# Up products with standing weights in fp32, read per block from memory, in place of split products with standing rows

## The chip, the cores and the metric

The kernel runs on one core of one Trainium2 chip. The metric is device time in microseconds (us), the median of several runs; a profiled execution gives the rows quoted below. TensorE is called PE, VectorE DVE, ScalarE ACT, GpSimd POOL, SyncE SP. A "block" is 128 token rows that one expert processes.

## What is computed

A cross attention is followed by a mixture of experts (8 experts, the best 2 for each token). Batch 16, 256 queries, 1601 keys, width 128, hidden width 256.

```python
x = x + attention(layernorm(x) @ Wq + bq, ctx @ Wk + bk, ctx @ Wv + bv, mask)
xn = rms_norm(layernorm(x), norm_scale)
weights, idx = softmax(top_k(xn @ w_router.T, 2))
up = xn @ w_up[idx].T            # [rows, 512], halves u and gate
h = u * silu(gate)
down = h @ w_down[idx].T         # [rows, 128]
x = layernorm(x) + sum(down * weights) + x
```

## The kernel before

**Two stages.** 32 units (128 queries of one batch each) of attention run first, in slots that interleave scores, exponentials, turns of the probabilities and products with the context. Each token's normalized row goes to memory twice, scattered by POOL into `rows_in`, one region for each expert (`scatter`, L570). Then NB = 71 blocks of 128 rows are read back, each from one expert's region; DVE works out the tables of which block belongs to which expert. The first 41 blocks (FULL) come from the first 24 units and can start before the last units are done. The last four slots of attention stand between the steps of blocks 0, 2, 5 and 8 (`LATE_SLOTS`).

**One step of the second stage**, in the order written for PE in `step(m)`: turn the rows of block m+1 (L1505), up products of block m (L1532), turn the hidden values of block m-2 (L1549), down products of block m-3 (L1560). PE takes the expert number of a block from a register and so addresses that expert's weights among all eight, which stay on the chip.

The up product stands the turned rows and moves 512 columns of weights, three times in the fast one-pass type (F32R): high rows by high weights, high rows by low weights, low rows by high weights. ACT makes the high part of the rows (L809) and DVE the low part (L1265). The weights were split in the same way once for each expert during attention (ACT L795, DVE L1036), from `wup_in`. After the up product ACT takes the tanh of the gate half (L819), DVE makes the hidden values in two instructions (L1287, L1292), PE turns them, ACT copies them out (L825), PE makes the down product, ACT scales it with the gate (L832) and POOL scatters it to `parts` (L643, semaphore `s_sent`).

**Order of the other engines.** Each engine runs its instructions in the order written. On DVE the tables for the second phase stand after the work of blocks 14 (`table_all`), 16 (`table_owners`) and 17 (`table_starts`), `find_places` after block 12. POOL has, between the sends of results, the last scatters of the attention: three before the send of block 6 and four before that of block 11.

**SP** issues the transfers: `load_block(m)` (L469) into a ring of XR = 12 buffers, so it first waits for `s_sent` of block m-12; after blocks 29 to 36 also `fill_end` (L447), and after blocks 64 to 69 the six loads of parts (`load_parts`, L483, 512 KB each), of which the first waits for the results of blocks 44 to 55. Every fourth block SP first loads four row numbers into registers (L465). At the end the last results are gathered, added and stored.

Of the kernel before, what the change touches and what calls it, by code (L numbers as in the profile page):

```python
# [28 lines left out]
P = 128  # L29
# [15 lines left out]
def xattn_moe(nc, x, ctx_rows, ctx_cols, mask, wq_t, wk_t, wv, bq, bk, bv, norm_scale, w_router_t,  # L45
# [67 lines left out]
    with st:  # L113
# [15 lines left out]
        wup_in = sb("wup_in", [P, H2])  # L129
# [3 lines left out]
        wup_high = sb("wup_high", [P, E, H2], F32R)  # L133
        wup_low = sb("wup_low", [P, E, H2], F32R)
# [99 lines left out]
        xt_high = sb("xt_high", [P, 2, P], F32R)  # L234
        xt_low = sb("xt_low", [P, 2, P], F32R)

        inner = mbias[:].rearrange("p a n -> p (a n)")[:, YR * D:YR * D + 4 * 2 * H].rearrange("p (s j h) -> p s j h", s=4, j=2)
        th, sg, hid, hid_t = inner[:, 0], inner[:, 1], inner[:, 2], inner[:, 3]
# [17 lines left out]
        s_wup = sem("up_weights_loaded")  # L256
        s_wup_high = sem("up_weights_high")
        s_wup_low = sem("up_weights_low")
# [39 lines left out]
        s_ht = sem("hidden_turned")  # L298
# [9 lines left out]
        s_xt_high = sem("block_turned_high")  # L308
        s_xt_low = sem("block_turned_low")
        s_htc = sem("hidden_turned_copied")  # L310
# [72 lines left out]
        def _(sp):  # L383
# [25 lines left out]
            def load_expert(e):  # L409

                wait(sp, s_wup_low, e)
                sp.dma_start(wup_in[:].unsqueeze(1), w_up_t[bass.ds(e, 1)].rearrange("e d h -> d e h")).then_inc(s_wup, 16)
# [20 lines left out]
            end_regs = [sp.alloc_register(f"row_end{e}") for e in range(E)]  # L433
            start_regs = [sp.alloc_register(f"start_row{k}") for k in range(CH)]
# [35 lines left out]

            def load_parts(u, n):
# [191 lines left out]
        def _(act):  # L663
# [69 lines left out]
            def even_slot(i, k):  # L733
# [14 lines left out]
                if k == 2 and is_unit(u):  # L748
                    split_up_weights(i)
# [40 lines left out]
            def split_up_weights(e):  # L790

                act.wait_ge(s_wup, 16 * (e + 1))
                if e == 0:
                    act.wait_ge(s_consts, N_CONSTS)
                act.activation(wup_high[:, bass.ds(e, 1)], wup_in[:].unsqueeze(1), ACT.Copy,  # L795
                               scale=norm_col[:]).then_inc(s_wup_high, 1)

# [6 lines left out]
            def block_xt(m):  # L804

                act.wait_ge(s_bxt, m + 1)

                wait(act, s_up, m - 1)
                act.activation(xt_high[:, m % 2], ps[:, 0, 0:P], ACT.Copy).then_inc(s_xt_high, 1)  # L809

            def step(m):
                if is_block(m + 1):
                    block_xt(m + 1)
# [6 lines left out]
                if is_block(m - 2):  # L820

                    act.wait_ge(s_ht, m - 1)

                    wait(act, s_down, m - 3)
                    act.activation(hid_t[:, m % 2], ps[:, 4 + m % 2, 0:HC * P], ACT.Copy).then_inc(s_htc, 1)  # L825
                if is_block(m - 3):

                    n = m - 3
# [6 lines left out]
            run(act, slot, lambda: block_xt(0), step)  # L835

        @block.vector
        def _(dve):
# [194 lines left out]
            def split_up_weights(e):  # L1033

                dve.wait_ge(s_wup_high, e + 1)
                dve.scalar_tensor_tensor(wup_low[:, bass.ds(e, 1)], wup_in[:].unsqueeze(1), norm_col[:],  # L1036
                                         wup_high[:, bass.ds(e, 1)].bitcast(F32), ALU.mult, ALU.subtract).then_inc(s_wup_low, 1)

# [9 lines left out]
            def even_slot(i, k):  # L1048
# [43 lines left out]
                if u == UNITS - 2:  # L1092
                    split_up_weights(i)
# [3 lines left out]
            def odd_slot(i, k):  # L1097
# [39 lines left out]
                if k == 3 and is_unit(u + 1):  # L1137
                    split_up_weights(i)
# [121 lines left out]
            def split_block(m):  # L1260

                dve.wait_ge(s_xt_high, m + 1)

                wait(dve, s_up, m - 1)
                dve.tensor_tensor(xt_low[:, m % 2], ps[:, 0, 0:P], xt_high[:, m % 2].bitcast(F32),  # L1265
                                  ALU.subtract).then_inc(s_xt_low, 1)

# [14 lines left out]
            def step(m):  # L1282
                if is_block(m + 1):
                    split_block(m + 1)
                if is_block(m):
# [5 lines left out]
                    wait(dve, s_ht, m - 1)  # L1291
# [14 lines left out]
            run(dve, slot, lambda: split_block(0), step)  # L1306
# [5 lines left out]
        def _(pe):  # L1312
# [187 lines left out]
            def turn_block(m):  # L1500
# [3 lines left out]
                wait(pe, s_xt_low, m)  # L1504
# [14 lines left out]
            def step(m):  # L1519
# [3 lines left out]
                if is_block(m + 1):  # L1523
                    turn_block(m + 1)
                if is_block(m):
                    e = expert(m)
                    pe.wait_ge(s_xt_low, m + 1)
# [83 lines left out]
```

## Time and profile before

| | us |
|---|---|
| median of 3 runs | 417.36 (416.56 to 419.87) |
| the profiled execution, its own time | 416.63 |
| its span | 414.9 |
| PE busy | 367.9 (89%) |
| PE weight loads busy | 340.7 (82%) |
| DVE busy | 319.6 (77%) |
| ACT busy | 272.7 (66%) |
| POOL busy | 222.8 (54%) |
| DMA queue of SP, share of 16 engines | 44.0% |

The span runs from the first to the last instruction of the profiled execution; its time has 1.7 us around the span. "Busy" counts every moment in which an engine has an instruction in work. Matmuls are pipelined, so busy PE is not PE at its peak. The chain that ended last (followed back from the last instruction, at each step to what released it) lies on PE for 82% of the span.

### The profile page before, as it was taken

What the parts mean: (1) busy time and instruction counts of PE and PEld (TensorE: products, weight loads), DVE (VectorE), ACT (ScalarE), POOL (GpSimd) and SP (SyncE); (2) the same over time, 40 slices, a digit from 0 to 9 for tenths busy, and PEclk for the clock granted to TensorE, in tenths of its full rate; (3) what the DMA queues carried; (4) which work ended last, traced back from release to release, by engine and by line L of the source; (5) the groups of instructions that cost most, each with busy time, mean ns of one, the idle gap of its engine ahead of it and who ended that gap; (6) DMA issues with size and microseconds to landing.
All of it is one profiled execution on the core that took longest, in us unless ns stands there. A gap on an engine that the chain in (4) does not pass through costs nothing.

```text
span 414.9 us, 9967 instructions
## 1 busy us (share of the span) xinstructions
PE 367.9 (89%) x2608; PEld 340.7 (82%) x2608; DVE 319.6 (77%) x1349; ACT 272.7 (66%) x646; POOL 222.8 (54%) x377
## 2 busy tenths in 40 slices
PE   2549999999999999999999999788968999999840
PEld 1449999999999999999999999676856888888630
DVE  2367888898898898898898899655687777777682
ACT  1135877778777777777777876645755777778630
POOL 1061223465666665666576474447677766666560
PEclk9999999999999999999999999988999999999975
DMA  4908736735844844765764660402232543335728
GB/s 140 297 28 290 214 107 222 261 100 219 276 123 195 277 150 181 263 149 190 255 211 148 235 182 21 92 14 59 66 85 83 137 105 92 91 85 161 279 65 278
DMA packets 57526, 66.65 MB, mean 161 GB/s; under 512 B 5856, under 2 KB 49136, under 8 KB 57472
## 3 DMA queue, kind: packets, MB, share of 16 engines
q1 hardware_dynamic: 53120, 56.99, 44.0%
q0 software_dynamic: 4320, 8.92, 6.4%
q8 instruction: 24, 0.39, 0.4%
q14 instruction: 30, 0.25, 0.2%
q10 hardware_dynamic: 32, 0.10, 0.1%
HBM read 53.88 MB, written 12.11 MB: 159 GB/s over the span
## 4 chain that ended last, share of the span: by engine, by line
PE 82%; DVE 5%; DMA 4%; issue 4%; ACT 2%; SPq 1%; POOL 1%; POOLq 0%; ACTq 0%; DVEq 0%
PE ps L1381 23%; PE ps L1346 17%; PE ps L1532 11%; PE ps L1363 11%; PE ps L1560 6%; PE ps L1549 3%; PE ps L1332 2%; PE ps L1505 2%; PE ps L1404 2%; DMA attention<-parts 1%; DMA blk_x<-rows_in 1%; DMA parts<-mbias,blk_x 1%; PE ps L1399 1%; PE ps L1326 1%; PE ps L1389 1%
## 5 line engine op out<-in xcount | busy, mean ns | idle before, releaser
L1381 PE MATMUL ps<-attention,ctx_sb 128*128 128x128 f32 (+1 forms) x832 | 107.6, 278 | 0.0
L1381 PEld LDWEIGHTS ps<-attention,ctx_sb 128*128 128x128 f32 (+1 forms) x832 | 99.0, 192 | 0.0
L643 POOL DMA_INDIRECT parts<-mbias,blk_x x71 | 70.5, 993 | 35.5 <-ACT mbias L832 27.9
L570 POOL DMA_INDIRECT rows_in<-kept,place x64 | 72.7, 1136 | 17.5 <-issue 17.5
L717 ACT ACTIVATE attention<-ps 128x512 f32<-128x512 f32 x96 | 55.5, 596 | 19.8 <-PE ps L1363 19.8
L912 DVE CUSTOM_DVE_ANT_0 attention<-ps,mbias 128x1608 f32<-128x1608 f32 x32 | 58.5, 1828 | 11.7 <-issue 10.9
L702 ACT ACTIVATE attention<-attention,ebias 128x1601 f32<-128x1601 f32 x32 | 52.3, 1635 | 18.7 <-DVE ebias L930 18.5
L1363 PE MATMUL ps<-ident,attention 128*128 128x128 f32 (+1 forms) x416 | 64.0, 275 | 0.4 <-ACT attention L717 0.4
L537 POOL TENSOR_TENSOR rstd<-ve,minus_half 128x2 f32<-128x2 f32 x32 | 22.9, 717 | 70.7 <-DVE ve L973 70.7
L1346 PE MATMUL ps<-ctxt_high,gt_high 128*128 128x402 f32 x128 | 51.1, 399 | 9.6 <-DVE wr_sb L1176 6.2
L1363 PEld LDWEIGHTS ps<-ident,attention 128*128 128x128 f32 (+1 forms) x416 | 51.2, 143 | 3.7 <-ACT attention L717 0.7
L1287 DVE SCALAR_TENSOR_TENSOR mbias<-mbias,ps 128x256 f32<-128x256 f32 x71 | 29.9, 421 | 28.7 <-ACT mbias L819 28.3
L1560 PE MATMUL ps<-wdn_sb,mbias 128*128 x284 | 45.7, 285 | 0.0
L1346 PE MATMUL ps<-ctxt_high,gt_low 128*128 128x402 f32 x128 | 45.5, 355 | 0.0
L1346 PE MATMUL ps<-ctxt_low,gt_high 128*128 128x402 f32 x128 | 45.3, 354 | 0.0
L819 ACT ACTIVATE mbias<-ps 128x256 f32<-128x256 f32 x71 | 27.3, 384 | 25.8 <-PE ps L1532 25.8
L1560 PEld LDWEIGHTS ps<-wdn_sb,mbias 128*128 128x128 f32 x284 | 38.4, 196 | 1.2 <-issue 0.4
L1532 PE MATMUL ps<-wup_high,xt_high 128*128 x71 | 35.6, 501 | 0.2
L527 POOL TENSOR_TENSOR rstd<-ve,minus_half 128x2 f32<-128x2 f32 x16 | 11.1, 693 | 44.9 <-DVE ve L863 44.9
L1346 PEld LDWEIGHTS ps<-ctxt_high,gt_high 128*128 128x128 f32 x128 | 25.2, 196 | 10.8 <-issue 10.8
L1292 DVE SCALAR_TENSOR_TENSOR mbias<-mbias,ps 128x256 f32<-128x256 f32 x71 | 29.9, 421 | 2.4
L1030 DVE TENSOR_TENSOR ctxt_low<-ctxt_in,ctxt_high 128x1601 fp32r<-128x1601 f32 x16 | 29.2, 1825 | 0.0
(149 smaller groups left out, 788.6 us busy)
## 6 DMA issues: line engine op xcount, KB each, us to landing
ctxt_in<-ctx_cols SPq DMA_DIRECT2D x16, 800.5 KB
mbias<-mbias_dram SPq DMA_DIRECT2D x16, 800.5 KB, 5.6
ctx_sb<-ctx_rows SPq DMA_DIRECT2D x16, 768.0 KB
blk_x<-rows_in SPq DMA_DIRECT2D x71, 65.0 KB, 2.1
attention<-parts SPq DMA_DIRECT2D x8, 512.0 KB, 6.0
x_in<-x SPq DMA_DIRECT2D x16, 128.0 KB, 2.2
wup_in<-w_up_t SPq DMA_DIRECT2D x8, 256.0 KB
out<-base_all SPq DMA_DIRECT2D x8, 256.0 KB, 5.4
```

Source lines behind the costliest of these rows:

```text
L570: pool.indirect_dma_start(rows_in, bass.IndirectOffsetOnAxis(ap=place[:, c, u:u + 1], axis=0), kept[:, u % KEPT, c], None).then_inc(s_scat ...
L643: pool.indirect_dma_start(parts, bass.IndirectOffsetOnAxis(ap=blk_x[:, m % XR, D:D + 1].bitcast(I32), axis=0), blk_y[:, m % YR], None).the ...
L702: act.activation(probs[:, k % 2], scores[:, 0:SK], ACT.Exp, bias=ebias[:, k:k + 1], scale=SCALE, accum_out=esum[:, k:k + 1]).then_inc(s_ex ...
L717: act.activation(probs_t[:, g * BANK:(g + 1) * BANK], ps_turn[:, g % 2], ACT.Copy).then_inc(s_pt_act, 1)
L912: dve.tensor_tensor_reduce(out=scores.rearrange("p (c w) -> p c w", c=SCORE_CHUNKS), in0=ps_scores, in1=mbias[:, j].rearrange("p (c w) -> ...
L1287: dve.scalar_tensor_tensor(sg[:, m % 2], th[:, m % 2], 1.0, ps[:, 2 + m % 2, H:H2], ALU.add, ALU.mult).then_inc(s_sg, 1)
L1292: dve.scalar_tensor_tensor(hid[:, m % 2], sg[:, m % 2], 0.5, ps[:, 2 + m % 2, 0:H], ALU.mult, ALU.mult).then_inc(s_h, 1)
L1346: last = pe.matmul(ps_scores[:, c], queries[:, j, (k % 2) * P:(k % 2 + 1) * P], keys[:, j, c * CW:(c + 1) * CW], start=m == 0, stop=m == l ...
L1363: last = pe.transpose(ps_turn[0:n, g % 2, (t - 4 * g) * P:(t - 4 * g + 1) * P], probs[:, k % 2, t * P:t * P + n], ident[:])
L1381: last = pe.matmul(ps_o[:, 0:P], ctx_sb[0:n, j, t], probs_t[0:n, t * P:(t + 1) * P], start=t == 0, stop=t == KT - 1)
L1532: last = pe.matmul(ps[:, 2 + m % 2], rows[:, m % 2], weights[:, bass.ds(e, 1)].rearrange("p a h -> p (a h)"), start=n == 0, stop=n == len( ...
L1560: last = pe.matmul(ps[:, (1, 6)[m % 2], 0:D], hid_t[:, (m - 3) % 2, c * P:(c + 1) * P], wdn_sb[:, bass.ds(e, 1), c].rearrange("p a d -> p ...
```

## The change

The up product stands 128 columns of weights and moves the 128 turned rows, four matmuls in plain fp32 for each block; its result has the hidden index on the partitions, so the turn of the hidden values and its copy fall away and the down product follows one step earlier. The rows are no longer split: ACT makes one copy, which also applies `norm_scale`, two blocks ahead (`AHEAD`). The weights are no longer kept on the chip: SP reads the 256 KB of the block's expert from memory into a ring of WR = 4 buffers, for block m-4 after it has issued the rows of block m. The splits of the weights and the eight loads of `wup_in` fall away.

```diff
+    WR = 4
+    LEAD = 4
+    AHEAD = 2
-        wup_in = sb("wup_in", [P, H2])
-        wup_high = sb("wup_high", [P, E, H2], F32R)
-        wup_low = sb("wup_low", [P, E, H2], F32R)
+        wup_sb = sb("wup_sb", [P, WR, H2])
-            for m in range(NB + 3):
+            for m in range(NB + 2):
 # SP
-                wait(sp, s_wup_low, e)
-                sp.dma_start(wup_in[:].unsqueeze(1), w_up_t[bass.ds(e, 1)]...).then_inc(s_wup, 16)
+            def load_up_weights(m):
+                k = m % CH
+                if k == 0 or m == FULL:
+                    n = min(CH - k, (FULL if m < FULL else NB) - m)
+                    sp.load(owner_regs[k:k + n], owner[0:1, m:m + n])
+                wait(sp, s_up, m - WR + 1)
+                e = sp.snap(owner_regs[k], min_val=0, max_val=E - 1)
+                sp.dma_start(wup_sb[:, m % WR].unsqueeze(1),
+                             w_up_t[bass.ds(e, 1)]...).then_inc(s_wup[m % WR], 16)
-            for m in range(NB):
+            for m in range(LEAD):
                 load_block(m)
+            for m in range(LEAD, NB):
+                load_block(m)
+                load_up_weights(m - LEAD)
                 if FILL_LOAD <= m < FILL_LOAD + E:
                     fill_end(m - FILL_LOAD)
                 n = m - PART_LOAD
                 if 0 <= n < FIRST_UNITS // CH:
                     load_parts(CH * n, CH)
+            for m in range(NB - LEAD, NB):
+                load_up_weights(m)
 # ACT
-            def split_up_weights(e):
...
-            def block_xt(m):
...
+            def copy_rows_t(m):
+                act.wait_ge(s_bxt, m + 1)
+                wait(act, s_up, m - AHEAD)
+                act.activation(rows_t[:, m % (AHEAD + 1)], ps[:, 0, 0:P], ACT.Copy, scale=norm_col[:]).then_inc(s_rows_t, 1)
-                    act.activation(hid_t[:, m % 2], ps[:, 4 + m % 2, 0:HC * P], ACT.Copy).then_inc(s_htc, 1)
 # DVE
-            def split_up_weights(e):
...
-            def split_block(m):
...
-                    wait(dve, s_ht, m - 1)
+                    wait(dve, s_down, m - 1)
 # PE
-                if is_block(m + 1):
-                    turn_block(m + 1)
+                if is_block(m + AHEAD):
+                    turn_block(m + AHEAD)
                 if is_block(m):
-                    pe.wait_ge(s_xt_low, m + 1)
+                    pe.wait_ge(s_rows_t, m + 1)
+                    pe.wait_ge(s_wup[m % WR], 16 * (m // WR + 1))
                     wait(pe, s_h, m - 1)
-                    products = ((xt_high, wup_high), (xt_high, wup_low), (xt_low, wup_high))
-                    for n, (rows, weights) in enumerate(products):
-                        last = pe.matmul(ps[:, 2 + m % 2], rows[:, m % 2], ...)
+                    for c in range(2 * HC):
+                        last = pe.matmul(ps[:, 2 + m % 2, c * P:(c + 1) * P],
+                                         wup_sb[:, m % WR, c * P:(c + 1) * P],
+                                         rows_t[:, m % (AHEAD + 1)], start=True, stop=True)
-                        last = pe.transpose(ps[:, 4 + m % 2, c * P:(c + 1) * P], hid[:, m % 2, c * P:(c + 1) * P], ident[:])
-                if is_block(m - 3):
+                if is_block(m - 2):
-                        last = pe.matmul(ps[:, (1, 6)[m % 2], 0:D], hid_t[:, (m - 3) % 2, c * P:(c + 1) * P],
+                        last = pe.matmul(ps[:, (1, 6)[m % 2], 0:D], hid[:, m % 2, c * P:(c + 1) * P],
             def before_steps():
-                pe.wait_ge(s_wup_low, E)
-                turn_block(0)
+                for m in range(AHEAD):
+                    turn_block(m)
```

## Rows read from the trace of the kernel before

**Rows 1.** Busy time of each engine by stretch, with granted clock and DMA share.
```profile
core 0: us, PE busy (x) PEld busy (x) DVE busy (x) ACT busy (x) POOL busy (x), PEclk, DMA share, GB/s
60.00:300.00 240.00, 233.76 (x1756) 223.72 (x1755) 203.23 (x1010) 173.65 (x366) 138.40 (x255) 0.99 0.53 171
...
340.00:350.00 10.00, 10.00 (x69) 8.79 (x69) 7.08 (x21) 7.82 (x26) 6.67 (x7) 1.00 0.35 92
```
**Rows 2.** Chain that ended last, second stage: start, length, what.
```profile
315.04 0.96 PE ps L1532 x3
...
354.61 0.72 PE ps L1532 x3
355.33 0.22 PE ps L1549 x2
355.55 0.45 PE ps L1560 x4
...
374.25 0.74 PE ps L1532 x3
```
**Rows 3.** Timeline 300 to 318: start, length, instruction, count, idle before and its releaser.
```profile
301.63 0.50 PE L1532 MATMUL ps<-wup_high,xt_high 128*128 x1
...
306.37 0.30 PE L1505 MATMUL ps<-ident,blk_x 128*128 128x128 f32 x1 [1.65 <-DVE xt_low L1265]
...
311.76 0.30 PE L1505 MATMUL ps<-ident,blk_x 128*128 128x128 f32 x1 [1.99 <-DVE xt_low L1265]
...
314.73 0.30 PE L1505 MATMUL ps<-ident,blk_x 128*128 128x128 f32 x1 [1.02 <-DVE xt_low L1265]
```
**Rows 4.** Timeline of POOL and of SP's queue in the same stretch.
```profile
300.58 0.97 POOL L643 DMA_INDIRECT parts<-mbias,blk_x  x1 [0.30 <-issue]
...
303.01 14.57 SPq L469 DMA_DIRECT2D blk_x<-rows_in  x8
...
314.94 1.28 SPq L469 DMA_DIRECT2D blk_x<-rows_in  x2
```
**Rows 5.** Chain that ended last, from a block's down product to the next transfers.
```profile
375.68 0.38 ACT mbias L832
...
376.32 2.25 DMA parts<-mbias,blk_x
378.77 0.33 SPq L483
```
**Rows 6.** Issue to landing of x_in (128 KB), over the whole span.
```profile
DMA to landing us min/median/max: 2.1/2.2/5.2
```
**Rows 7.** DMA view of 376 to 392: queue, and issues with us to landing.
```profile
q1 hardware_dynamic: 1728, 3.55, 63.3%
...
...
blk_x<-rows_in SPq DMA_DIRECT2D x6, 65.0 KB, 5.4
```
**Rows 8.** Chain of waits in attention, products with the context.
```profile
259.95 1.79 PE ps L1381 x16
```
**Rows 9.** Start of the second stage: SP's fifth block, PE's first up product.
```profile
L469 SPq DMA_DIRECT2D blk_x<-rows_in x1: 333/333/333, 263.2 to 263.2; - x1
...
265.65 0.49 PE L1532 MATMUL ps<-wup_high,xt_high 128*128 x1
```
**Rows 10.** SP's queue: a fill and the block after it; a register load.
```profile
323.56 0.36 SPq L447 DMA_DIRECT2D rows_in<-filler  x1
324.11 0.34 SPq L469 DMA_DIRECT2D blk_x<-rows_in  x1
...
L465 SPq TENSOR_LOAD <-start_row x1: 303/303/303, 262.8 to 262.8; - x1
```
**Rows 11.** Chain that ended last, last block.
```profile
394.67 0.96 PE ps L1532 x3
...
398.05 0.38 ACT mbias L832
```
**Rows 12.** Busy time by stretch, same columns as rows 1.
```profile
275.00:280.00 5.00, 3.84 (x17) 2.99 (x16) 3.58 (x24) 2.93 (x9) 1.65 (x4) 0.74 0.00 2
```

More of the change, by code:

```diff
@@ L255, in xattn_moe @@
         s_wdn = sem("down_weights_loaded")
[L256 to L258 removed]
+        s_wup = [sem(f"up_weights_loaded{j}") for j in range(WR)]
         s_mbias = [sem(f"mbias_loaded{j}") for j in range(2)]
@@ L433, in _ @@
             end_regs = [sp.alloc_register(f"row_end{e}") for e in range(E)]
+            owner_regs = [sp.alloc_register(f"block_owner{k}") for k in range(CH)]
             start_regs = [sp.alloc_register(f"start_row{k}") for k in range(CH)]
@@ L801, in _, with before_steps @@
             split_ctxt(0, 1)
-            def block_xt(m):
+            def copy_rows_t(m):
                 act.wait_ge(s_bxt, m + 1)
-                wait(act, s_up, m - 1)
-                act.activation(xt_high[:, m % 2], ps[:, 0, 0:P], ACT.Copy).then_inc(s_xt_high, 1)
+                if m == 0:
+                    act.wait_ge(s_consts, N_CONSTS)
+                wait(act, s_up, m - AHEAD)
+                act.activation(rows_t[:, m % (AHEAD + 1)], ps[:, 0, 0:P], ACT.Copy, scale=norm_col[:]).then_inc(s_rows_t, 1)
+            def before_steps():
+                for m in range(AHEAD):
+                    copy_rows_t(m)
             def step(m):
-                if is_block(m + 1):
-                    block_xt(m + 1)
+                if is_block(m + AHEAD):
+                    copy_rows_t(m + AHEAD)
                 if is_block(m):
@@ L833, in step @@
                                    scale=blk_x[:, n % XR, D + 1:D + 2]).then_inc(s_y2, 1)
-            run(act, slot, lambda: block_xt(0), step)
+            run(act, slot, before_steps, step)
         @block.vector
@@ L1304, in step @@
                     (sum_choices, add_base)[n // 2 % 2](n // 4)
-            run(dve, slot, lambda: split_block(0), step)
+            run(dve, slot, lambda: None, step)
             for n in range(SUMMED_EARLY, 2 * (UNITS // CH)):
@@ L1502, in turn_block @@
                 pe.wait_ge(s_blk[m % XR], 16 * (m // XR + 1))
-                wait(pe, s_xt_low, m)
+                wait(pe, s_rows_t, m)
                 pe.transpose(ps[:, 0, 0:P], blk_x[:, m % XR, 0:D], ident[:]).then_inc(s_bxt, 1)
@@ L1522, in step @@
                     pe.wait_ge(s_owner, PHASES)
-                if is_block(m + 1):
-                    turn_block(m + 1)
+                if is_block(m + AHEAD):
+                    turn_block(m + AHEAD)
                 if is_block(m):
-                    e = expert(m)
-                    pe.wait_ge(s_xt_low, m + 1)
+                    pe.wait_ge(s_rows_t, m + 1)
+                    pe.wait_ge(s_wup[m % WR], 16 * (m // WR + 1))
                     wait(pe, s_h, m - 1)
-                    products = ((xt_high, wup_high), (xt_high, wup_low), (xt_low, wup_high))
-                    for n, (rows, weights) in enumerate(products):
-                        last = pe.matmul(ps[:, 2 + m % 2], rows[:, m % 2],
-                                         weights[:, bass.ds(e, 1)].rearrange("p a h -> p (a h)"), start=n == 0,
-                                         stop=n == len(products) - 1)
+                    for c in range(2 * HC):
+                        last = pe.matmul(ps[:, 2 + m % 2, c * P:(c + 1) * P],
+                                         wup_sb[:, m % WR, c * P:(c + 1) * P],
+                                         rows_t[:, m % (AHEAD + 1)], start=True, stop=True)
                     last.then_inc(s_up, 1)
@@ L1574, in before_steps @@
                 load_owners(0)
-                turn_block(0)
+                for m in range(AHEAD):
+                    turn_block(m)
             run(pe, slot, before_steps, step)
```

50 lines of the change are left out of this document (8 added, 42 removed).

## The prediction

> **What bounds the kernel now.** I read the busy time by stretch first. In attention PE is busy 233.8 of 240 us [rows 1]; the splits of the weights that go away there, on ACT, DVE and the DMA queues, lie beside it. I cost their removal at nothing: PE covers them. Everything happens in the second stage.
>
> The chain in order of time shows what a step there is made of: up 0.72, turn of the hidden values 0.22, down 0.45, and 0.11 for the turn of the next rows, which merges into the gap before the next up product (354.61 to 356.11 is one step) [rows 2]. To number the blocks: DVE's `table_starts` ends step 17, so the turn at 314.73 belongs to step 19 and the up product at 315.04 to block 19; 39 steps on, that at 374.25 is block 58. A step is (374.25 - 315.04)/39 = 1.518 us, and PE never stops in it: it is the bound.
>
> Before that stretch it is not. In the timeline from 300 to 318 PE's turn waits three times for DVE's low part of the rows, which stands behind the tables in DVE's order: 1.65, 1.99 and 1.02 us [rows 3]. And POOL is late: the result of block 6 is sent at 300.58, when PE is about to do block 14 (301.63), so SP can issue the rows of block 18 only at 303.01 and those of block 23 (sixth of the following eight) at 314.94 [rows 3, 4]. Twelve row buffers hide this lag today.
>
> **The sum, part by part** (against the profiled execution, 416.63 with a span of 414.9; the median is 0.7 above it).
>
> *Prices.* In attention 16 records of plain fp32 matmul with 128 columns take 1.79 us, 0.112 each, their weight loads hidden [rows 8]. Four matmuls of the new up product are 8 such records: 0.90 in place of 0.72. The 256 KB of weights are in no measured issue; 128 KB of x land in 2.1 to 2.2 us when the queue is free, 65 KB of rows behind parts in 5.4 [rows 6, 7]. At the rate found below (0.35 MB/us) 128 KB are 0.37 us, so a landing has a fixed 1.8; with 0.75 for 256 KB and 0.19 for the rows ahead of them I take 2.7 in a free queue (nearest to the x load). Ends 2.2 and 5.4. One more transfer costs SP 0.55 from start to start, a register load 0.3 [rows 10].
>
> *Step.* 0.11 + 0.90 + 0.45 = 1.46 against 0.11 + 0.72 + 0.22 + 0.45 = 1.50; measured 1.518, so with the same remainder 1.485. Over blocks 21 to 60: 39 x 0.033 = **-1.3**. DVE loses its split (0.3 a step) and ACT a copy; neither was the bound, so nothing. ACT's copy now scales too, same shape, nothing. The new wait of DVE for the down product of two blocks ago is met while ACT does the tanh: nothing.
>
> *Start.* SP issues the fifth block at 263.2; the weights of block 0 stand behind it and a register load: issue 263.25 + 0.55 + 0.3 = 264.1, landing 266.8. PE starts its first up product at 265.65 [rows 9]. The rest of attention's last slots is queued behind it on PE: **+1.2**.
>
> *Weights behind the late sends.* The weights of block j are issued behind the rows of block j+4, which wait for the result of block j-8. So only 8 blocks, not 12, may lie between POOL and PE. With POOL's order and times kept: weights of block 14 land at 303.01 + 0.55 + 2.7 = 306.3, PE wanted them at 301.63: +4.6. Block 19: 314.94 + 3.25 = 318.2 against 315.04, +3.2. From there steps of 1.49: block 21 at 321.2 against 315.04 + 2 x 1.518 = 318.1. The waits for tables disappear inside these (PE no longer waits for the low part, only for hidden values, one step later). **+3.1** in place of a gain.
>
> *Fills.* In the eight steps of blocks 29 to 36 SP has three transfers each, 3 x 0.54 + 0.15 for two register loads in four = 1.77 a step, over 1.485: 8 x 0.29 = 2.3, less the lead of about 1 us that the weights have by then: **+1.2**. In a plain step it has 1.25 and keeps up.
>
> *Steady lead.* From the end of a block's down product to SP's next issue it takes 378.77 - 375.68 + 0.03 = 3.1 us [rows 5]. After the change down of block n ends 2 steps + 1.35 after its up begins; its rows' successor is issued at 2T + 4.45, the weights at 2T + 5.0 (5.3 with the register load), landing 2T + 8.0, needed at 8T. With T = 1.485: 11.0 against 11.9. Met, with 0.9 to spare; nothing.
>
> *Parts.* The first load of parts waits for block 55, thus is issued when block 60 begins on PE. Each of the six stands before the rows and weights of later blocks: the weights of block 66 stand behind all six. The queue moved 3.55 MB (six parts, six blocks' rows) in 63.3% of 16 us = 10.1 us of all engines, 0.35 MB/us [rows 7]. At that rate six blocks' weights, 1.57 MB, add 4.5 us and seven scatters of 65 KB 1.3; the fixed part of a landing is 1.8. Up of block 66 at 17.7 after block 60, block 70 four steps on: 23.6. Before it was 394.67 - (374.25 + 2 x 1.518) = 17.4 [rows 2, 11]. That is +6.2; if the queue does 0.4 MB/us, +4.3. I take **+5.5**, nearer to the measured rate.
>
> *End.* From the last up product to the last scaled result it is 398.43 - 394.67 = 3.75 [rows 11]; after: 0.90, tanh 0.38, two on DVE 0.87, down 0.45, scaling 0.38 and four handovers: 3.15. **-0.6**.
>
> Sum: -1.3 + 1.2 + 3.1 + 1.2 + 5.5 - 0.6 = **+9.1**, so 416.6 + 9.1 = **425.7 us**.
>
> **Rivals.**
> *Steady lead used up.* With the weights, the DMA share of a step goes from 0.35 [rows 1] by 0.26/0.35 = 0.75 us to (0.53 + 0.75)/1.485 = 0.86. If scatter and weights then land 1.6 us later together, T must satisfy 8T >= 2T + 9.6: 1.60, and 39 x 0.115 = 4.5 more: **430**. For: with parts in the queue 65 KB took 5.4 us, where 128 KB take 2.2 in a free one [rows 6, 7]. Against: 0.86 is not full. The Trainium skill (DMA: Bandwidth & Descriptors, "Latency and other measured facts") gives HBM latency as 0.2 us on average and 2 us at high load; by its upper figure this rival would be the forecast, and no trace here shows it in a plain step. Chance 0.17.
> *The clock falls.* In 275 to 280, after waits of PE in the late slots, the granted clock was 0.74 [rows 12], that is 2.6 of 5 us at 1.2 GHz, 1.3 us lost. The waits of block 14, 19 and 61 would be longer (3 to 5 us); three falls of that kind, one or two in places where PE is the bound, and slower matmuls around them: +3, **429**. The waits of 1.0 to 2.0 us [rows 3] brought no fall. The Trainium skill (TensorE: Matmul & The Clock Gate, Part 1) has the array at half rate after idling, so by it at least the start and block 14 would see one. Chance 0.11.
> *Parts cost little.* If the transfers are interleaved so that weights overtake the parts, and the fills hide in the lead: +1.2 + 3.1 - 1.3 - 0.6 + 1 = +3.4, **420**. Against: nothing in the queue's order says so. Chance 0.13.
> *Faster: the table waits go and the weights are there in time.* One mechanism: PE's dependence on DVE's low part. Its three waits are 4.66 us; each gets one step (1.49) of slack, 0.16 + 0.5 are left, so -4.0; with the step and the end -5.9: **411**. It decides if SP issues block 18's rows before about 298, so that block 14's weights land in time; POOL's late slots and scatters fix it at 303. It needs POOL to send block 6 five us earlier. Chance 0.07.
> *No real product saved.* The change trades 0.72 + 0.22 for 0.90; were a record 0.14, PE's step is 1.68 and the time 433. Against: 0.112 over 16 records. Chance 0.04.
> Forecast 0.48.
>
> **Numbers.** About 1% is what a measurement of this kernel tells from no change: 413.2 and 421.5. Faster: the fourth rival, 0.08. Within: most of the third and a bit of the forecast's lower end, 0.15. Slower: 0.77. Range 419.5 to 432: below it the faster rival and a part of the third, above it the dearest ends of the first, second and fifth.
>
> **What would show it.** The chain after should name the transfer of the weights at the first up product, around blocks 13 to 15 and 19, and from block 61 on; block 14's up product should start about 4.6 to 6 us later than today. The eight up records should take 0.90, and plain steps 1.485. SP should still issue the rows of block 18 between 303 and 305. From block 60 to 70: about 23 us. Waits of PE's turn for DVE should be gone. I am wrong if weights never appear as what PE waits for, if POOL's sends come early, or if plain steps are over 1.55.

## The result, and the profile after

The changed kernel takes 435.02 us (median of 4 runs, 434.0 to 437.98); the kernel before, run beside it on the same chip, 417.75 (416.56 to 419.87). The ratio is 1.042, 95% interval 1.035 to 1.049: slower, by about twice what was forecast and outside the range. The profiled run took 435.8 us with a span of 434.1, against 416.63 and 414.9.

The page of the kernel after: first busy time, granted clock and DMA share in 40 slices; then the queues; then a group of instructions (busy us, mean ns, idle before it); then DMA issues (KB each, us from issue to landing).

```profile
PE 371.0 (85%) x2821; PEld 354.8 (82%) x2821; DVE 298.1 (69%) x1270; ACT 253.3 (58%) x567; POOL 219.0 (50%) x377
...
PE   2559999999999999999999997876867889885850
...
DMA  3907753674485377448646506346678878778928
...
L1512 PE MATMUL ps<-rows_t,wup_sb 128*128 128x128 f32 x568 | 81.7, 289 | 23.2 <-ACT rows_t L812 10.6
...
wup_sb<-w_up_t SPq DMA_DIRECT2D x71, 256.0 KB, 3.4
...
blk_x<-rows_in SPq DMA_DIRECT2D x71, 65.0 KB, 3.1
```

Attention (the nines of the PE row) is as it was. From the second stage on PE has idle slices, where DMA stands at 7 or 8 tenths, and 23.2 us of idle time stand before the up product.

The chain of waits of the kernel after, start, length and what: the start of the second stage, blocks 13 and 14 (301.38, 305.48), block 21 (321.43), plain steps around block 40, the part where the partial results are loaded, and the end.

```profile
262.66 2.69 DMA wup_sb<-w_up_t
265.49 1.14 PE ps L1512 x8
...
301.38 1.74 PE ps L1512 x8
303.12 0.87 PE ps L1528 x4
...
305.48 2.06 PE ps L1512 x8
...
321.43 1.13 PE ps L1512 x8
...
354.90 0.89 PE ps L1512 x8
355.79 0.45 PE ps L1528 x4
356.35 0.89 PE ps L1512 x8
...
370.67 1.13 PE ps L1512 x8
...
415.61 0.89 PE ps L1512 x8
...
423.12 5.71 DMA attention<-parts
```

These lines stand beside [rows 2, 9, 11] of the kernel before. The eight records of an up product take 0.89 us, the four of a down product 0.45: the step's own work is as priced. But from 356.35 (block 40) to 370.67 (block 48) go 14.32 us, 1.79 a step, where before it was 1.518. In this chain each product that had to wait takes 1.13 in place of 0.89 (at a granted clock of 1.00), so a wait costs 0.24 us more than its idle time.

Busy time by stretch, columns as in [rows 1]: kernel after, around block 14, plain steps, and parts.

```profile
300.00:310.00 10.00, 7.32 (x40) 6.98 (x41) 3.47 (x11) 2.40 (x7) 7.70 (x8) 0.66 0.74 218
...
345.00:375.00 30.00, 27.50 (x232) 25.83 (x232) 14.58 (x35) 17.47 (x53) 17.08 (x18) 1.00 0.78 227
394.00:410.00 16.00, 10.70 (x67) 9.94 (x68) 4.70 (x12) 5.35 (x17) 5.27 (x6) 0.79 1.02 373
```

And the DMA view of 350 to 375, issue to landing in the last column, first the kernel after, then the kernel before in the same stretch:

```profile
q1 hardware_dynamic: 4201, 4.71, 67.4%
...
wup_sb<-w_up_t SPq DMA_DIRECT2D x15, 256.0 KB, 3.3
blk_x<-rows_in SPq DMA_DIRECT2D x15, 65.0 KB, 3.2
parts<-mbias,blk_x POOLq DMA_INDIRECT x15, 3.6
```
```profile
q1 hardware_dynamic: 2404, 1.11, 19.8%
...
blk_x<-rows_in SPq DMA_DIRECT2D x17, 65.0 KB, 1.9
parts<-mbias,blk_x POOLq DMA_INDIRECT x18, 2.3
```

The DMA share went from 0.34 to 0.78 (345 to 375 in both), and rows and scatters land 1.3 us later, though the queues are not full. Only from 394 on, with parts, are they full (1.02).

**Where the 19.2 us of span went**, by the starts of the up products of single blocks (counted out in the trace, eight records a block; us from the span's start):

| kernel | block 8 | 21 | 37 | 60 | 70 | end of span | a step 21-37 | a step 37-60 | 60 to 70 |
|---|---|---|---|---|---|---|---|---|---|
| before | 291.3 | 318.1 | 342.3 | 377.0 | 394.7 | 414.9 | 1.51 | 1.51 | 17.7 |
| after | 289.5 | 321.4 | 351.2 | 392.1 | 415.4 | 434.1 | 1.86 | 1.78 | 23.3 |
| ring of 8 | | 322.0 | 351.7 | 391.1 | 413.9 | 432.1 | 1.86 | 1.71 | 22.8 |
| ring of 8, no lead | 292.4 | 318.4 | 349.6 | 383.1 | 405.0 | 423.2 | 1.95 | 1.46 | 21.9 |
| 16 row buffers | 290.8 | 315.5 | 345.0 | 378.7 | 402.1 | 420.3 | 1.85 | 1.46 | 23.4 |
| half of the bytes | | 322.0 | 349.5 | 386.0 | 407.8 | 426.0 | 1.72 | 1.59 | 21.8 |
| no reads | 288.7 | 315.1 | 339.8 | 373.1 | 390.2 | 408.3 | 1.54 | 1.45 | 17.1 |
| deep and ordered | 291.1 | 316.3 | 341.6 | 374.9 | 389.2 | 408.1 | 1.58 | 1.45 | 14.3 |

Kernel after against before: +3.3 by block 21, +5.6 in 21 to 37 (with the fills), +6.2 in 37 to 60, +5.6 in 60 to 70, and -1.5 behind block 70's up product. So 11.8 of the 19.2 us are in the steps that the forecast had at -0.1. Each line of the table is one profiled run: three kernels that do the same in blocks 37 to 60 (16 row buffers, and two variants of it below) give 1.46, 1.53 and 1.51 a step there, so a difference under about 0.08 a step tells nothing.

### The profile page after: what moved, and what is told of

Read it like the earlier page. It is cut to its first block, busy times and chain, and to the rows that moved or that the text cites. A ratio compares the mean times of both kernels' runs of the same rounds, so it can differ in the third digit from the quotient of the medians.

```text
span 434.1 us, 10039 instructions
## 1 busy us (share of the span) xinstructions
PE 371.0 (85%) x2821; PEld 354.8 (82%) x2821; DVE 298.1 (69%) x1270; ACT 253.3 (58%) x567; POOL 219.0 (50%) x377
## 4 chain that ended last, share of the span: by engine, by line
PE 75%; issue 9%; DVE 9%; DMA 2%; ACT 2%; SPq 1%; POOL 1%; ACTq 0%; DVEq 0%; POOLq 0%
PE ps L1362 20%; PE ps L1512 17%; PE ps L1327 14%; PE ps L1344 9%; PE ps L1528 7%; PE ps L1313 2%; PE ps L1486 1%; PE ps L1385 1%; DMA attention<-parts 1%; ACT rows_t L812 1%; PE ps L1307 1%; PE ps L1370 1%; DVE base_all L1262 1%; PE ps L1380 1%; DVE xn L873 1%
## 5 line engine op out<-in xcount | busy, mean ns | idle before, releaser
L1512 PE MATMUL ps<-rows_t,wup_sb 128*128 128x128 f32 x568 | 81.7, 289 | 23.2 <-ACT rows_t L812 10.6
L1512 PEld LDWEIGHTS ps<-rows_t,wup_sb 128*128 128x128 f32 x568 | 72.9, 201 | 30.6 <-issue 15.7
L913 DVE CUSTOM_DVE_ANT_0 attention<-ps,mbias 128x1608 f32<-128x1608 f32 x32 | 58.5, 1827 | 12.7 <-issue 11.5
L548 POOL TENSOR_TENSOR rstd<-ve,minus_half 128x2 f32<-128x2 f32 x32 | 22.9, 714 | 72.0 <-DVE ve L974 72.0
L1528 PEld LDWEIGHTS ps<-wdn_sb,mbias 128*128 128x128 f32 x284 | 39.6, 202 | 0.8 <-issue 0.8
```

Source lines behind the costliest of these rows:

```text
L913: dve.tensor_tensor_reduce(out=scores.rearrange("p (c w) -> p c w", c=SCORE_CHUNKS), in0=ps_scores, in1=mbias[:, j].rearrange("p (c w) -> ...
L1512: last = pe.matmul(ps[:, 2 + m % 2, c * P:(c + 1) * P], wup_sb[:, m % WR, c * P:(c + 1) * P], rows_t[:, m % (AHEAD + 1)], start=True, stop ...
L1528: last = pe.matmul(ps[:, (1, 6)[m % 2], 0:D], hid[:, m % 2, c * P:(c + 1) * P], wdn_sb[:, bass.ds(e, 1), c].rearrange("p a d -> p (a d)"), ...
```

## The experiments

### The ring or the lead: which of the two

**Theory.** In plain steps the weights come late, because they stand behind rows that wait for the result of the block eight earlier; the loop of those eight blocks is longer than eight steps. **Rivals:** the ring of four weight buffers is too short, or the queues can't carry the bytes in time.

Ring of eight buffers alone:

```diff
-    WR = 4
+    WR = 8
```

> The changed kernel with a ring of 8 weight buffers in place of 4, the order of SP's queue as it was (weights of block m-4 behind the rows of block m). Theory L (lead): the weights of block j wait in SP's queue behind the rows of block j+4 and so for the send of block j-8; the ring's size is not what holds them. Then blocks 21 to 60 stay at 1.81 us a step (1.75 to 1.85) and the time at 433 to 436. Rival R (ring): four buffers are too few, the load waits for an up product; then the step falls to about 1.5 and the time to about 423. Rival B (bandwidth): unchanged too, 1.81.

Measured: 434.39 us, ratio to the kernel before 1.0437 (1.037 to 1.0504). Nothing is gained; the steps are 1.86 and 1.71, against 1.86 and 1.78. The ring is not what holds PE in plain steps.

The same ring, and weights issued with their own block's rows, which wait for the result of block j-12 instead of j-8:

```diff
-    WR = 4
-    LEAD = 4
+    WR = 8
+    LEAD = 0
```

> A ring of 8, and the weights of block m issued behind the rows of block m itself (LEAD 0), so they wait for the send of block m-12 and the up product of block m-8. Same bytes as the change. Theory L: plain steps fall from 1.81 to about 1.50 (39 steps: -12), the waits before blocks 13 to 15 and 19 shrink (-3 to -5), blocks 60 to 70 stay at about 23 us; time about 418 to 421. Rival B (the DMA engines cannot bring 256 KB more a step): the step stays over 1.7 and the time over 430. In between (1.55 to 1.65) both have a part.

Measured: 423.45 us, 1.0148 (1.0057 to 1.0239).

Twelve blocks of lag for the weights by four more row buffers, ring and lead untouched:

```diff
-    XR = 12
+    XR = 16
```

> The changed kernel with 16 row buffers in place of 12 (ring of 4 weights, order as it was): the weights of block j now wait for the send of block j-12 and the up product of block j-4, their lead being at most about 4 steps. Theory L: step about 1.50 to 1.55, time 419 to 424. Rival B: step over 1.7, time over 430. Rival R (ring of 4 too small): step over 1.6.

Measured: 422.98 us, 1.0163 (1.0093 to 1.0233). Two edits that share only the distance to the awaited result (12 blocks) give the same 12 us. In blocks 37 to 60 they also agree one by one (33.5 and 33.7 us, where the changed kernel takes 40.9); in the rest they do not, since no lead loses 1.3 us in 21 to 37 and 16 row buffers gain 2.9 us more by block 21. The stretches of 345 to 375 of the two, first no lead, then 16 row buffers:

```profile
345.00:375.00 30.00, 30.00 (x270) 29.82 (x269) 17.32 (x42) 20.98 (x63) 19.50 (x21) 1.00 0.90 278
```
```profile
345.00:375.00 30.00, 29.97 (x268) 29.71 (x267) 17.41 (x42) 20.82 (x63) 19.72 (x21) 1.00 0.93 274
```

The queues carry more (0.90 and 0.93, against 0.78) and PE does not stop once. That excludes the queues' throughput as the bound of a plain step: the share of 0.78 was the result of the slow steps, not their cause. The steps of 21 to 37 did not get shorter in either, but for different reasons. Without lead one wait makes up most of PE's idle time of 326 to 340, first as a row of the waits (us, times, longest), then in the chain:

```profile
PE ps L1486 <- DMA blk_x<-rows_in: 2.9, 1, 2.9
...
327.89 5.63 DMA blk_x<-rows_in
```

PE's turn of block 30's rows, which stands ahead of block 28's product in its order, waits for rows issued 5.6 us before; blocks 28 to 30 start 4.7, 2.8 and 2.8 us after the one before, at a granted clock that fell (0.83 over 325 to 345), so a part of these steps is the clock. In the kernel with 16 row buffers it is the weights: from their issue to the product go 3.9 to 5.6 us in blocks 26 to 29, with the ring of four behind them.

The same lag in the kernel before, where no weights are read: eight row buffers.

```diff
-    XR = 12
+    XR = 8
```

> The kernel before, with 8 row buffers in place of 12, no other change. It has the change's distance of 8 blocks to the send, on the 65 KB of rows alone. Theory L: the rows of block 14 wait for the send of block 6 (303) and land at 305; PE waits about 4 us there and about 1 to 2 at block 19, so blocks 8 to 21 take about 30 instead of 26.8; plain steps: 2.9 + 9.2 us against 8 steps of 1.51 = 12.1, just met, 1.51 to 1.56; time 418 to 423. Rival B: no lead is needed, time within 1 of before.

Measured: 454.74 and 447.49 us in two runs, so 31 to 38 us over the 416.48 of the kernel before beside it; the two differ by 1.6%, so no ratio is given. The waits of 286 to 440 (us in total, times, longest):

```profile
PE ps L1505 <- DMA blk_x<-rows_in: 28.3, 21, 4.1
```

418 to 423 was expected; the loss is five to six times the largest that this allowed. The median landings of 350 to 375 are those of the kernel before (rows 1.9, scatters 2.3 us), yet a step of 37 to 60 takes 2.13. The expectation compared the loop with eight steps, but not all of them are in it. This kernel makes the down product of block n in step n+3, and turns the rows of block n+8, which wait for it, at the start of step n+7, where the down product of block n+4 stands: so the loop goes round once in four steps. One round of it in the chain of this run goes from the turn at 356.01 to the one at 364.79: the step's own work 1.98, scaling and the way to the scatter 0.67, scatter 3.99, SP 0.16, rows 1.93, handover 0.04, in all 8.8 us for four blocks, 2.19 each. The granted clock fell too (0.89 over 345 to 375). In the changed kernel the down product stands in step n+2 and the weights are needed only at the product of block n+8, so its loop goes round once in six steps, and it loses less. The lines of this kernel are from the longer of the two runs.

### The bytes

**Theory.** The loop's landings grow with the share of the queues, so fewer bytes shorten the step even with the lag of eight. **Rival:** the lag alone, with landings as in a free queue. Half of the weights read, the second half of the products reading the first half's columns again:

```diff
-                sp.dma_start(wup_sb[:, m % WR].unsqueeze(1),
+                sp.dma_start(wup_sb[:, m % WR, 0:H].unsqueeze(1),
...
-                                         wup_sb[:, m % WR, c * P:(c + 1) * P],
+                                         wup_sb[:, m % WR, c % HC * P:(c % HC + 1) * P],
```

> The changed kernel, but each block reads only the first 256 of 512 columns of its weights and the products use them twice (half of the weights are left out of the computation). 128 KB in place of 256 KB. Theory B: engine time a step falls from about 1.37 to 1.0 us, the step to PE's 1.46 to 1.50. Theory L: landings of weights about 0.5 to 0.8 shorter and those of the scatter back towards 2.4, so 6T = 10.8 - 1.9, the step 1.50 to 1.60. Blocks 60 to 70 fall from 23.3 to about 20. Time 419 to 424.

Measured: 428.33 us, 1.0292 (1.0225 to 1.0358), dearer than the 419 to 424 expected. Its DMA view of 350 to 375:

```profile
wup_sb<-w_up_t SPq DMA_DIRECT2D x15, 128.0 KB, 2.3
blk_x<-rows_in SPq DMA_DIRECT2D x16, 65.0 KB, 2.7
parts<-mbias,blk_x POOLq DMA_INDIRECT x16, 2.8
```

Each landing is 0.5 to 1.0 us shorter than with all bytes, and the plain step 1.59 instead of 1.78. By the loop the two landings in it, weights and scatter, save 1.0 + 0.8 = 1.8 us over six steps, 0.30 a step expected, 0.19 found (the profiled run is one; other waits lie around them).

No reads at all: the eight experts' weights loaded once, in attention, and each product reading a fixed one of them:

```diff
-        wup_sb = sb("wup_sb", [P, WR, H2])
+        wup_sb = sb("wup_sb", [P, E, H2])
...
-                load_up_weights(m - LEAD)
...
-                                         wup_sb[:, m % WR, c * P:(c + 1) * P],
+                                         wup_sb[:, m % E, c * P:(c + 1) * P],
```

> The changed kernel with all eight experts' fp32 up weights kept on the chip (loaded during attention) and no reads per block; the up product takes the weights of expert m mod 8 in place of the block's own, so the choice of the expert in the up product is left out. All instructions on PE, ACT and DVE are those of the change. This is the change without its reads. Theory L and B alike: everything that was lost is in the reads. Plain steps 1.45 (PE alone, as in the runs with more lead), the table waits mostly gone (block 8 to 21 about 23, was 26.8 before and 31.9 after), blocks 60 to 70 about 16, time about 406 to 410. Rival P (the rearranged products themselves are slower): step over 1.5, time over 415.

Measured: 409.45 us, 0.9796 (0.9696 to 0.9895). Without its reads the change is worth 2% (7 us by the medians), within the 406 to 410 expected, and the reads cost 25.8 us of span (434.1 - 408.3): 6.3 by block 21, 12.7 in 21 to 60, 6.2 in 60 to 70, and 0.6 behind it. By block 21 it is 3.0 us ahead of the kernel before; in blocks 37 to 60 it gains 1.4 and loses 0.5 in 21 to 37.

One part of its expectation failed: blocks 8 to 21 were to take about 23 us, with the waits for tables mostly gone, and take 26.4. Between 300 and 322 this kernel too has PE idle for 6 us, and what is left there is not the weights. The chain shows what sets block 21:

```profile
309.84 2.24 DMA parts<-mbias,blk_x
...
312.57 2.22 DMA blk_x<-rows_in
```

Block 11's late send (309.84) frees the buffer for block 23's rows, and PE turns these before block 21's product because the change turns two blocks ahead. So with 12 row buffers only 10 blocks lie between the awaited result and that turn, and block 21 starts at 315.1 without any weights to wait for. With 16 row buffers it comes no earlier (315.5); what stands there then was not followed up.

### Fills, parts, and their order

16 row buffers and the fills issued on ACT's queue, steps 22 to 29, so that SP has two transfers a step there and not three:

```diff
-    XR = 12
+    XR = 16
...
-                if FILL_LOAD <= m < FILL_LOAD + E:
-                    fill_end(m - FILL_LOAD)
...
+                if FILL_STEP <= m < FILL_STEP + E:
+                    fill_end(m - FILL_STEP)
...
```

> As the run with 16 row buffers, the eight fills issued from ACT's queue at steps 22 to 29 in place of SP's. Same bytes. In the 16-buffer run blocks 21 to 37 still took 1.85 a step, and 37 to 60 only 1.46. Theory S (SP's issue: three transfers and the register loads, 1.77 us a step or more): blocks 21 to 37 fall to 1.5 to 1.6, time 418 to 419. Theory F (the fills fill the DMA engines, share 0.9 there): they stay at 1.75 to 1.85, time unchanged at 422 to 424.

Measured: 420.75 us, 1.0095 (1.0053 to 1.0137), which overlaps with the interval of 16 row buffers alone; steps of 21 to 37 take 1.77 against 1.85. SP's issue time is at most a small part of that stretch. (The 1.85 is itself uncertain: the next kernel, which differs from 16 row buffers only after that stretch, has 1.89.)

16 row buffers and the six loads of parts behind the last weights:

```diff
-    SUMMED_EARLY = 2
+    SUMMED_EARLY = 0
...
-                n = m - PART_LOAD
-                if 0 <= n < FIRST_UNITS // CH:
-                    load_parts(CH * n, CH)
...
+            for n in range(FIRST_UNITS // CH):
+                load_parts(CH * n, CH)
```

> As the run with 16 row buffers, the six loads of parts (3.1 MB) issued behind all weights in place of between them, the early sums dropped from the steps. Theory Q (the weights of blocks 61 to 70 stand behind the parts in one queue): blocks 60 to 70 fall from 23.4 to 15 to 17, and 2 to 4 of it come back at the end, where parts and sums are later; time 416 to 420. Rival: the late sums cost as much as is gained, 422 to 424.

Measured: 417.14 us, 0.9989 (0.9939 to 1.0039), against 1.0163 with parts in the old place, intervals apart. Blocks 60 to 70 take 15.1 us instead of 23.4. Its SP queue (start, length, count) shows the parts issued when the last weights are out. From block 70's product to the end it takes 2.9 us more (21.1 against 18.2), so 5.4 of the 8.3 remain.

```profile
384.27 6.12 SPq L474 DMA_DIRECT2D wup_sb<-w_up_t  x5
...
390.99 3.46 SPq L489 DMA_DIRECT2D attention<-parts  x6
```

16 row buffers and half of the bytes (the same edits as above, together):

```diff
-    XR = 12
+    XR = 16
...
-                sp.dma_start(wup_sb[:, m % WR].unsqueeze(1),
+                sp.dma_start(wup_sb[:, m % WR, 0:H].unsqueeze(1),
...
```

> As the run with 16 row buffers, reading only the first 256 of 512 columns of the weights and using them twice (half of the weights are left out). With the lead given, the bytes are told from it. Theory F (fills and weights fill the DMA engines in blocks 21 to 37): 1.85 a step falls to 1.50 to 1.60. If SP's issue is the bound there it stays over 1.75. Blocks 60 to 70: 20 to 22 (22 in the half-byte run without the lead). Time 414 to 418.

Measured: 418.77 us, 1.0074 (1.0047 to 1.0101). Plain steps 1.46, as with all bytes; steps of 21 to 37 are 1.73, between the 1.50 to 1.60 expected if the bytes were the bound there and the over 1.75 if SP's issue was. Half of the bytes takes at most 0.12 to 0.16 off a step there and doesn't free the stretch with the fills.

All of it together: 16 row buffers, ring of eight, no lead, parts last, fills on ACT:

```diff
-    XR = 12
+    XR = 16
...
-    WR = 4
-    LEAD = 4
+    WR = 8
+    LEAD = 0
...
-    SUMMED_EARLY = 2
+    SUMMED_EARLY = 0
...
+                if FILL_STEP <= m < FILL_STEP + E:
+                    fill_end(m - FILL_STEP)
...
+            for n in range(FIRST_UNITS // CH):
+                load_parts(CH * n, CH)
...
```

> The reads kept, all remedies together: 16 row buffers, 8 weight buffers with LEAD 0, the fills on ACT's queue, the parts behind all weights. Theory L with Q: blocks 37 to 60 at 1.45, 60 to 70 about 15, blocks 21 to 37 at 1.6 to 1.8 because there the fills and the weights together fill the DMA engines; time 412 to 416. If the fills' stretch was SP's issue or a late ring instead: 21 to 37 at 1.5 and 409 to 411.

Measured: 409.56 us, 0.9836 (0.9798 to 0.9875): 1.6% faster than the kernel before, and faster than the changed one, with every byte of the 71 x 256 KB read. By stretch:

```profile
325.00:345.00 20.00, 19.95 (x179) 19.79 (x178) 11.40 (x28) 13.80 (x42) 15.00 (x16) 1.00 0.90 272
345.00:375.00 30.00, 30.00 (x271) 30.00 (x270) 17.29 (x42) 20.75 (x63) 20.19 (x21) 1.00 0.95 286
```

and the chain of a step, then the end:

```profile
346.07 0.89 PE ps L1514 x8
346.96 0.45 PE ps L1530 x4
347.41 0.11 PE ps L1488
...
396.83 5.38 DMA attention<-parts
```

The weights land in 3.7 us there, rows in 4.1 and scatters in 4.3 (medians of 350 to 375), later than in the changed kernel, and it costs nothing in that stretch, where PE never stops: the landings are covered, at a DMA share of 0.95. The stretch 21 to 37 fell to 1.58 a step.

The same with the fills back on SP, the lines of the changed kernel:

```diff
-    FILL_STEP = 22
+    FILL_LOAD = FULL - E - 4
```

> As the run with all remedies (16 row buffers, 8 weight buffers, LEAD 0, parts last), but the eight fills back in SP's queue between the blocks. It tells what made blocks 21 to 37 fast there (1.58 a step, against 1.85 with 16 row buffers and a ring of 4). If the deeper ring of weights did it (their landing takes 4 to 5.6 us in that stretch and a ring of 4 gives them 4): 21 to 37 stays at 1.55 to 1.65 and the time at 409 to 411. If taking the fills out of SP's queue did it: 1.75 to 1.9 and 412 to 415.

Measured: 410.74 us, 0.985 (0.9742 to 0.9959); steps of 21 to 37 take 1.63. No difference from the last one that a measurement can tell. What freed the stretch with the fills is therefore ring, lead and rows together: the rows alone leave the weights short, the ring without lead leaves the rows short, and each of the two kernels showed that wait. In this kernel the weights also wait for the result of 16 blocks earlier in place of 12, so ring and distance were not told apart there.

### Another way to the same products

The eight experts' weights resident, and the block's copied on the chip into a ring of three, one half by DVE and one by ACT, two blocks ahead:

```diff
+        wup_ring = sb("wup_ring", [P, CR, H2])
...
+                act.activation(wup_ring[:, m % CR, H:H2].unsqueeze(1), wup_sb[:, bass.ds(e, 1), H:H2], ACT.Copy).then_inc(s_wact, 1)
...
+                dve.tensor_copy(wup_ring[:, m % CR, 0:H].unsqueeze(1), wup_sb[:, bass.ds(e, 1), 0:H]).then_inc(s_wdve, 1)
...
-                                         wup_sb[:, m % WR, c * P:(c + 1) * P],
+                                         wup_ring[:, m % CR, c * P:(c + 1) * P],
```

> The changed kernel with all experts' fp32 up weights kept on the chip and, in place of the reads per block, a copy of the block's expert into a ring of three by DVE (first 256 columns) and ACT (last 256) two blocks ahead, the expert from a register of each. No DMA for it; everything is computed. Theory L: as the run without reads, if the copies fit: ACT has 1.02 us of work in a step of 1.45 and gets about 0.3 to 0.4, DVE has 0.87 and gets 0.2 to 0.6. Then steps 1.45 to 1.55 and 409 to 413. Rival: the two engines become the bound (DVE over 1.5, and its tables delay the copies): steps 1.6, 415 to 420.

Measured: 414.1 us, 0.9949 (0.9924 to 0.9974). Groups of 335 to 370 (busy us, mean ns | idle before):

```profile
L1541 PE MATMUL ps<-rows_t,wup_ring 128*128 128x128 f32 x183 | 25.1, 280 | 0.2 <-ACT wup_ring L805 0.2
...
L805 ACT ACTIVATE wup_ring<-wup_sb 128x256 f32 x23 | 9.5, 411 | 1.0 <-issue 0.5
L1271 DVE COPY wup_ring<-wup_sb 128x256 f32 x23 | 7.4, 320 | 1.2 <-PE ps L1541 0.6
```

The copies are nearly free in the plain stretch (PE waits 0.2 us for them), but the step is 1.55 there, not 1.45; the waits do not account for the 0.1 us, and its cause stays open. It is faster than the kernel before by half a per cent, and slower than the reads with enough buffers.

## Why the prediction was right in direction and wrong in size

**Step: right.** 0.89 + 0.45 + 0.11 = 1.45 in the chain of the kernel with all remedies; 1.485 was forecast with a remainder that is not there once nothing waits. The kernel without reads confirms it: 1.45 a step in blocks 37 to 60, where the kernel before takes 1.51.

**Steady lead: wrong, and this is the step that failed.** It said "11.0 against 11.9. Met, with 0.9 to spare; nothing." The loop was the right one; its landings were priced at too low a load, the scatter's from [rows 5] (2.25 us), the weights' at 2.7 "in a free queue". The prediction's own sign of being wrong, plain steps over 1.55, came true. One turn of it can be read off. Block 40's product starts at 356.35 and its result is sent at 361.77; SP issues the successor's rows at 366.08 and the weights behind them at 366.93, and block 48's product starts at 370.67. POOL's and SP's lines, timeline of the kernel after:

```profile
361.77 0.97 POOL L654 DMA_INDIRECT parts<-mbias,blk_x  x1 [0.48 <-ACT mbias L833]
...
365.24 0.33 SPq L474 DMA_DIRECT2D wup_sb<-w_up_t  x1
366.08 0.33 SPq L463 DMA_DIRECT2D blk_x<-rows_in  x1
366.93 0.33 SPq L474 DMA_DIRECT2D wup_sb<-w_up_t  x1
```

Two steps on PE are 3.40 of it (356.35 to 359.75) and up and down product 1.34. From the down product's end (361.09) to SP's issue it was 4.99 us where 3.1 [rows 5] stood in the sum, and from the weights' issue to the product 3.74 where 2.7 stood; rows to weights with a register load 0.85, as forecast. Of the 1.9 us more up to SP's issue, 1.35 are the scatter, which landed 3.6 us after 361.77 and not 2.25; it was there at 365.4, and the other 0.5 is SP itself, still issuing block 47's weights (365.24) and then loading registers for block 52's rows. The 1.0 us more behind it is the landing of the weights. With those two steps as 2T, 8T = 2T + 1.34 + 4.99 + 0.85 + 3.74, so 6T = 10.92 and T = 1.82, where eight steps took 1.79 on average; the forecast had 8.0, T at least 1.33. The error of 2.9 us in the loop (scatter 1.4, weights 1.0, SP 0.5) turned a spare into 0.3 us in each step. Over blocks 21 to 60 that is 11.8 us in place of -0.1.

The rival "steady lead used up" had this mechanism, with 1.6 us more of landings and T = 1.60 (2.4 us were measured in the turn above); it had the right sign and place at a chance of 0.17, and its price was still too small. It argued against itself with "0.86 is not full". That was the wrong test: the landings of rows and scatters grew by 1.3 us at a share of 0.78. The sentence cited there from the Trainium skill (DMA: Bandwidth & Descriptors, "Latency and other measured facts"), 2 us of HBM latency at high load against 0.2, gave the direction; the rows and scatters here, which land 1.3 us later, agree in direction, while no run here shows the latency of the memory by itself.

**Weights behind late sends: right in mechanism at block 14, right at block 21 by luck.** Block 14 started at 305.48 (forecast 306.3) by the chain above, 3.9 us later than before, where 4.6 to 6 was the sign named. SP issued block 14's weights at 302.16, behind the rows of block 18 (301.63, not between 303 and 305); they took 3.3 to the product and not 2.7. Block 21 started at 321.43 (321.2), but on the way block 19 started at 315.96, 2.2 us before its forecast, and from there to block 21 it took 5.5 us and not 3.0. One reason for that is one that the prediction had ruled out ("The waits for tables disappear inside these"): before block 20 PE waits for hidden values that stand behind the tables in DVE's order.

```profile
316.67 0.91 DVE start_f L1243
...
318.16 0.43 DVE mbias L1273
...
318.73 1.13 PE ps L1512 x8
```

Block 21 itself then waits for weights issued at 318.63. Two errors of over 2 us cancelled. More lag (16 rows, no lead) brought block 21 to 315.5 and 318.4, no reads to 315.1. The sum also added the start's +1.2 on top, though with POOL's times kept, as this term assumes, the start would not have moved block 14.

**Start: wrong, small.** 265.49 instead of 266.8, no loss. SP issued the first weights 1.4 us earlier than assumed; the landing took the 2.69 that was taken (2.7).

**Fills: wrong in kind, the number by luck.** +1.2 was a price for SP's issue time. Steps of 21 to 37 are 1.86, 0.08 above the plain ones, so 1.3 us in all, but on top of the slow steps. Taking SP's third transfer away changed them little (1.85 to 1.77; 1.63 to 1.58). Ring, lead and rows together did it, since waits of up to 5.6 us from issue to use there overrun either alone. How much of the changed kernel's own 1.86 is each was not separated.

**Parts: right.** 23.3 us from block 60 to 70, where 17.4 + 5.5 = 22.9 was taken and 23.6 was its upper value, at a DMA share of 1.02. Moved behind the weights it is 15.1.

**End: right sign.** From block 70's product to its scaled result it went from 4.4 to 3.7 us, -0.7 (forecast -0.6; the 398.05 of [rows 11] was the scaling of block 69, so that the 3.75 stood for 4.4). What follows is another 0.8 shorter, not forecast.

**Clock: small.** It was 0.66 in 300 to 310 and 0.79 in 394 to 410. Blocks 13 and 14 have products of 1.74, 0.87 and 2.06 us in place of 0.89, 0.45 and 1.13, which is the lower level of 1.2 GHz after idle PE, 2.2 us lost. Both stretches are ones in which POOL's sends or the parts set the pace, so how much of the 2.2 us is in the total was not told apart. The rival "the clock falls" had the falls right, and part of its price. In plain steps it stayed at 1.00, so the waits there brought no fall.

**A lesson in reading.** The waits of the kernel after, 255 to 435, name the weights for little time.

```profile
PE ps L1512 <- ACT rows_t L812: 10.6, 11, 1.4
PE ps L1512 <- issue: 9.5, 11, 3.1
...
PE ps L1512 <- DMA wup_sb<-w_up_t: 1.2, 2, 0.9
```

Block m's product doesn't need the copy of the rows that stands there (it is that of block m+2, and PE's order merely puts its turn ahead of the product). The kernel without reads has the same copies and steps of 1.45, so the 10.6 us are not theirs. "Met" by this table would have been the wrong verdict a second time.

**What stays open.** 0.3 us a step of the loop was explained by its landings; why half of the bytes gave only 0.19 back was not. By the order of the tables (the first 41 blocks go through the 8 experts once) most blocks have the same expert as the one before, so most reads are of weights that are already there; leaving them out was not tried.

## What to carry to other kernels

When a new transfer is queued behind one that waits for a result, write down the whole loop: which result, how many blocks earlier, and every landing in it, and price the landings at the load that the change itself creates, not at the one of the trace of before. Count which steps are really in the loop: those from the result to the place in PE's order where the awaited data is first touched. Then buy blocks of lag (buffers) until the loop is covered with a microsecond or two per landing to spare: here four more row buffers, or the issue four blocks earlier, gave 12 us, and a deeper ring alone gave nothing. Large loads that nobody needs yet belong behind the small ones that the next block waits for.

## What the runs showed of the hardware

- Issue to landing grew well before the queues were full (medians of 350 to 375, shares of 345 to 375): 65 KB of rows took 1.9 us at a share of 0.34 (kernel before), 2.7 at 0.57 (half of the bytes), 3.2 at 0.78 (changed kernel) and 4.1 at 0.95 (all remedies); the indirect write of 65 KB 2.3, 2.8, 3.6 and 4.3. 256 KB of weights took 3.3 at 0.78 and 3.7 at 0.95, and the first block's 2.7. The share alone does not fix the landing: with 16 row buffers, at 0.93, rows took 3.4 and the indirect write 3.3.
- The DMA engines were busy for 0.95 of 30 us (286 GB/s) with PE never idle (all remedies).
- A product of eight fp32 records took 0.89 us in the chain when PE came from other work and 1.13 when it had waited.
- A copy of 128x256 fp32 within the chip's memory (`wup_sb` to `wup_ring`) took 0.32 us on DVE and 0.41 on ACT.
